# Last feed-forward of a transformer kernel: the turns of the last two z in other PSUM banks, products split in high and low parts, the last tile in halves

## The chip, the core and the metric

The kernel runs on one NeuronCore of a Trainium2 chip. Its time is the device time of one execution in microseconds (us). Five engines work side by side, each on a queue of its own, and meet in semaphores: TensorE (PE in the profile, with PEld for its weight loads), VectorE (DVE), ScalarE (ACT), GpSimd (POOL) and SyncE (SP), which here issues DMAs.

## What is computed

1,024 tokens of width 256 go through two pre-norm transformer layers. The change touches only the end, the second feed-forward, a pair of "bitlinear" layers around a GELU:

```python
def bitlinear(x, w):
    xn = layer_norm(x)
    x_hat = absmax_quant(xn)       # clip(xn * 128 / gamma, -128 + EPS, 128 - EPS) * gamma / 128
    w_hat = ternarize_weights(w)   # -g, 0 or +g
    return einsum('bsd,od->bso', x_hat, w_hat)
y = layernorm(x)
h = gelu(bitlinear(y, w_fc))       # 256 -> 1024
x = x + bitlinear(h, w_proj)       # 1024 -> 256
```

The quantisation does not round, so the operand of the product stays an fp32 number. The kernel splits it into a 16-bit high part and a 16-bit low part and multiplies both with the ternary weights.

## The kernel before, around the change

The tokens are NT = 8 tiles of 128. For each tile t the second feed-forward is this chain, and all of it is written out by hand, as one fixed order for each engine:

- `fc(t)` on PE: eight 128x512 products into banks 0 and 1 (t even) or 2 and 3 (t odd). It waits for the GELU of tile t - 2, which empties these banks.
- `gelu_of(t)` on ACT: GELU out of the two banks, with the row sum kept. It writes `gelu[:, t % 2]` and so waits until `squares(t - 2)` has read it.
- `z_mean(t)` on POOL, then `centre(t)` on ACT: `z[:, t % 2]` = gelu minus its mean. `squares(t)` on ACT: the sum of squares, which `z_factor(t)` on POOL turns into the scale of the result.
- `quantise_z(t)` on DVE: four instructions, absolute maximum, scale, reciprocal, and the product clipped from above, in place in z.
- `z_transposes(t)` on PE, called the turn of z(t) here: eight 128x128 transposes into banks 4 and 5, always these two. So it waits for `zT_lo_done` of tile t - 1, the last reader of the banks.
- `z_high(t)` on ACT copies banks 4 and 5 to `zT_hi[:, t % 2]` as fp16. `z_low(t)` on DVE takes the banks again, clips from below and subtracts the high part: `zT_lo[:, t % 2]`.
- `pj(t)` on PE: sixteen 128x256 products, high and low by turns, into bank 6 or 7 by the list RING. It waits for `zT_lo_done` of tile t before the first of them.
- `result(t)` on DVE: scaled product plus the residual. SP then stores the tile.

The order on PE in the last stage:

```python
z_transposes(0); fc(2); fc(3)
pe.wait_ge(gelu_done, 4)
x_transposes(3, 1, 0)              # tiles 4 to 7 of y, banks 2 and 3
for t in range(1, NT):
    z_transposes(t)
    side(STEPS + 3, f"pj{t - 1}")  # pj(t - 1)
    if t + 3 < NT: fc(t + 3)
side(STEPS + 3, f"pj{NT - 1}")
```

`x_transposes(3, 1, 0)` needs `quantise(1)` on DVE, the quantisation of y  for tiles 4 to 7, part of what the change calls the outer norm. `y_low(1, 2)` is its low part, and `fc(4)` to `fc(7)` need it. On DVE the order is `quantise(1)`, `quantise_z(1)`, `z_low(0)`, `y_low(1, 2)`, and then for t from 2 on `quantise_z(t)`, `z_low(t - 1)`, `result(t - 2)`. ACT runs for t from 3 on `centre(t)`, `gelu_of(t + 1)`, `z_high(t - 1)`, `squares(t)`.

The turns are line L1616 of the profile, all products L1248 (a helper), `x_transposes` L1264, `z_high` L774, `gelu_of` L782, `centre` L790, `squares` L797, `quantise_z` L1203 to L1207, `z_low` L1187, `y_low` L1180, `quantise` L1160 to L1165, `result` L1196, and `z_factor` L545 to L553.

Of the kernel before, what the change touches and what calls it, by code (L numbers as in the profile page):

```python
# [19 lines left out]
ALU = mybir.AluOpType  # L20
# [3 lines left out]
P = 128  # L24
# [3 lines left out]
Q_B = 128.0  # L28
# [3 lines left out]
def transformer_program(nc, x_in, wq_a, wk_a, wv_a, wo_a, w_gate_up, w_down,  # L32
                        wq_b, wk_b, wv_b, wo_b, w_fc, w_proj, cos_in, sin_in, out):
    T, C = x_in.shape[1], x_in.shape[2]
    NT = T // P
    KC = C // P
    F = w_down.shape[1]
    NF = F // P
# [16 lines left out]
    identf = sb("identf", 24, [P], F32)  # L55
# [36 lines left out]
    pjT = sb("pjT", 100.5, [KC, NF, P], F16)  # L92
# [41 lines left out]
    z = sb("z", 146, [2, F], F32)  # L134
    zT_hi = sb("zT_hi", 154, [2, NF, P], F16)
    zT_lo = sb("zT_lo", 158, [2, NF, P], F16)
# [30 lines left out]
    with ExitStack() as ctx:  # L167
        PS = ctx.enter_context(nc.psum_tensor("PS", [P, 8 * BANK], F32))

        def bank(b, n=1):  # L170
            return PS[:, b * BANK:(b + n) * BANK]
# [92 lines left out]
        STEPS = 8 * NG  # L264
# [9 lines left out]
        def blocks(G, part):  # L274
            r = of_step(G)[3]
            return 4 - r if part else 5 + r

        def q_tile(G, part):
            return blocks(G, part) - 1
# [42 lines left out]
        def side_bank(G, name):  # L322
            return 6 + RING.index((G, name)) % 2
# [250 lines left out]
        def _(act):  # L574
            def x_high(st, hf, c, b):

                act.wait_ge(xT_done, 4 * st + 2 * hf + c + 1)
                dst = (yT_hi if st == 3 else xnT_hi)[:, c, hf * BANK:(hf + 1) * BANK]
                nc.scalar.copy(dst, bank(b)).then_inc(xT_hi_done, 1)
# [191 lines left out]

            def z_high(t):
                act.wait_ge(zT_done, t + 1)
                nc.scalar.copy(zT_hi[:, t % 2], bank(4, 2).rearrange("p (i n) -> p i n", i=NF)).then_inc(zT_hi_done, 1)  # L774

            def gelu_of(t):

                act.wait_ge(fc_done, t + 1)
                act.wait_ge(gelu_scale_done, t // 4 + 1)
                if t >= 2:  # L780
                    act.wait_ge(z_squares_done, t - 1)
                nc.scalar.activation(gelu[:, t % 2, :], bank(2 * (t % 2), 2), ACT.Gelu, scale=bit[:, 3, t:t + 1],  # L782
                                     accum_out=bit[:, 8, t:t + 1]).then_inc(gelu_done, 1)
# [8 lines left out]

            def squares(t):

                if t:
                    act.wait_ge(z_squares_done, t)
                nc.scalar.activation(square[:], gelu[:, t % 2, :], ACT.Square, bias=bit[:, 9, t:t + 1],  # L797
                                     accum_out=bit[:, 10, t:t + 1]).then_inc(z_squares_done, 1)
# [15 lines left out]
            squares(2)  # L814
            for c in range(KC):
                x_high(3, 1, c, 2 + c)
            z_high(1)
            for t in range(3, NT):
                centre(t)
                if t + 1 < NT:  # L820
                    gelu_of(t + 1)
                z_high(t - 1)
                squares(t)
            z_high(NT - 1)


        @block.vector
        def _(dve):
# [322 lines left out]
            def y_centre(t):  # L1151
                dve.wait_ge(moments_done, 3 * NT + t + 1)
                nc.vector.tensor_scalar(y[:, t, :], x[:, TAIL_TILES[t], :], mean_of(3, t), None,
                                        ALU.subtract).then_inc(y_centred, 1)
# [29 lines left out]
            def z_low(t):  # L1184

                dve.wait_ge(zT_hi_done, t + 1)
                nc.vector.scalar_tensor_tensor(out=zT_lo[:, t % 2], in0=bank(4, 2).rearrange("p (i n) -> p i n", i=NF),  # L1187
                                               scalar=-Q_B, in1=zT_hi[:, t % 2], op0=ALU.max,
                                               op1=ALU.subtract).then_inc(zT_lo_done, 1)

            def result(t):
# [34 lines left out]
            tail_moments(7)  # L1226
            y_centre(6)
            y_centre(7)
            quantise(1)
            quantise_z(1)  # L1230
            z_low(0)
            y_low(1, 2)
            gelu_scale(1)
            for t in range(2, NT):
                quantise_z(t)
                z_low(t - 1)
                result(t - 2)
            z_low(NT - 1)
            result(NT - 2)
            result(NT - 1)  # L1240

# [2 lines left out]
        def _(pe):  # L1244
# [365 lines left out]

            def z_transposes(t):
                pe.wait_ge(z_done, t + 1)
                if t >= 1:
                    pe.wait_ge(zT_lo_done, t)
                for i in range(NF):
                    last = nc.tensor.transpose(bank(4, 2)[:, i * P:(i + 1) * P], z[:, t % 2, i * P:(i + 1) * P],  # L1616
                                               identf[:])
                last.then_inc(zT_done, 1)

            def pj(t, b):  # L1620
                pe.wait_ge(zT_lo_done, t + 1)
                product(bank(b)[:, 0:C], [(zT[:, t % 2, i, :], pjT[:, :, i, :])
                                          for i in range(NF) for zT in (zT_hi, zT_lo)]).then_inc(pj_done, 1)

            for G in range(STEPS):
                scores(G, 0)
# [17 lines left out]
            z_transposes(0)  # L1644
            fc(2)
            fc(3)
            pe.wait_ge(gelu_done, 4)
            x_transposes(3, 1, 0)
            for t in range(1, NT):
                z_transposes(t)  # L1650
                side(STEPS + 3, f"pj{t - 1}")
                if t + 3 < NT:
                    fc(t + 3)
            side(STEPS + 3, f"pj{NT - 1}")


# [33 lines left out]
```

## Time and profile before

| | us |
|---|---|
| median of 3 runs (616.26 to 617.71) | 616.76 |
| the profiled execution, its own time | 617.08 |
| its span, first to last instruction | 615.3 |
| the stretch of the span from the first turn of z(1) to the end | 579.17 to 615.3 |

The trace is of one execution. All positions are microseconds from the start of its span. In rows of a timeline the first two columns are start and duration, and the bracket is how long the engine was idle before, and what ended this. Durations of successive instructions can overlap a little. A matmul's end is modelled. In rows of the view by stretches, each engine has its busy time and its count of instructions in that stretch, and PEclk is the clock that was granted to TensorE, 1.00 for 2.4 GHz and 0.50 for 1.2 GHz.

### The profile page before, as it was taken

To read this page: it belongs to the slowest core of one execution; us is meant where nothing else is said; L and a number is where in the kernel's file an instruction comes from. 1 tells how busy PE (TensorE), PEld (TensorE's weight loads), DVE (VectorE), ACT (ScalarE), POOL (GpSimd) and SP (SyncE) were. 2 spreads that over 40 slices of the span, in tenths; PEclk is the share of its full clock that TensorE was granted. 3 is DMA by queue.
4 is the path that set the end of the run, shared out by engine and by line. 5 is a ranking of instruction groups with operands and counts; after the bars stand their busy time and mean duration, and the time that the engine had idled before them with its cause. 6 is when DMAs were issued, how large, how long until landed. Compare 5 with 4: busy or idle time off the path is not lost.

```text
span 615.3 us, 16325 instructions
## 1 busy us (share of the span) xinstructions
PE 560.4 (91%) x6880; PEld 484.4 (79%) x6880; DVE 458.6 (75%) x750; ACT 436.2 (71%) x607; POOL 451.6 (73%) x371
## 2 busy tenths in 40 slices
PE   5999999988979999999999999999999987978796
PEld 4878898976758888888878889888888876866474
DVE  4686767767767878777877888788788775765985
ACT  0624302168787889889779898888988888874684
POOL 3034336438997998998999899899999887872332
PEclk9999999998998999999999999999999999997799
DMA  8160004008999999999999999999999999994011
GB/s 286 58 205 0 2 23 89 2 2 145 202 163 187 180 183 207 194 189 179 210 188 191 207 191 203 196 186 211 186 188 182 199 207 189 183 195 88 1 34 36
DMA packets 317193, 91.76 MB, mean 149 GB/s; under 512 B 305984, under 2 KB 316224, under 8 KB 317120
## 3 DMA queue, kind: packets, MB, share of 16 engines
q1 hardware_dynamic: 311680, 86.66, 81.2%
q10 hardware_dynamic: 5440, 4.06, 2.6%
q8 instruction: 54, 0.88, 0.6%
q14 instruction: 19, 0.16, 0.1%
HBM read 13.11 MB, written 1.05 MB: 23 GB/s over the span
## 4 chain that ended last, share of the span: by engine, by line
PE 33%; POOL 24%; DMA 13%; DVE 13%; ACT 7%; SPq 5%; issue 5%; POOLq 0%; ACTq 0%; DVEq 0%
POOL p_lo L497 17%; DMA pT_lo<-p_lo 12%; PE PS L1248 10%; PE PS L1507 4%; DVE small L1078 4%; PE PS L1381 3%; POOL roped L486 3%; SPq L398 3%; PE PS L1527 3%; ACT probs L711 2%; PE PS L1358 2%; PE PS L1363 2%; PE PS L1359 2%; SPq L402 2%; POOL roped L483 2%
## 5 line engine op out<-in xcount | busy, mean ns | idle before, releaser
L497 POOL TENSOR_TENSOR p_lo<-probs,p_hi 128x2048 f16<-128x2048 f32 (+7 forms) x128 | 304.3, 2400 | 34.8 <-DMA pT_lo<-p_lo 20.3
L711 ACT ACTIVATE probs<-PS,small 128x128 f32<-128x128 f32 (+7 forms) x256 | 173.5, 743 | 46.0 <-DVE small L1078 42.7
L1078 DVE TENSOR_REDUCE small<-PS 128x2 f32<-128x2048 f32 (+7 forms) x128 | 172.7, 1350 | 20.9 <-PE PS L1507 20.3
L720 ACT CAST p_hi<-probs 128x2048 f16<-128x2048 f32 (+7 forms) x128 | 145.9, 1161 | 3.8 <-DMA pT_hi<-p_hi 3.8
L1527 PE MATMUL PS<-v_hi,pT_hi 128*128 128x65 f16 x1152 | 78.7, 195 | 2.1 <-DMA pT_hi<-p_hi 2.1
L1531 PE MATMUL PS<-v_lo,pT_hi 128*128 128x64 f16 x1152 | 78.6, 195 | 0.0
L1507 PE MATMUL PS<-k_hi,q_hi 64*128 64x512 f32 (+3 forms) x384 | 74.8, 385 | 2.9 <-ACT probs L711 2.9
L1527 PEld LDWEIGHTS PS<-v_hi,pT_hi 128*128 128x128 f16 x1152 | 73.8, 99 | 3.8 <-issue 2.2
L1531 PEld LDWEIGHTS PS<-v_lo,pT_hi 128*128 128x128 f16 x1152 | 72.4, 98 | 0.6
L1507 PE MATMUL PS<-k_lo,q_hi 64*128 64x512 f32 (+3 forms) x384 | 67.2, 344 | 0.0
L1507 PE MATMUL PS<-k_hi,q_lo 64*128 64x512 f32 (+3 forms) x384 | 66.9, 343 | 0.0
L1248 PE MATMUL PS<-wkq_hi,xnT_hi 128*128 128x320 f32 x128 | 44.1, 344 | 9.2 <-DVE t_sin L1026 3.0
L1527 PE MATMUL PS<-v_hi,pT_lo 128*128 128x65 f16 x1152 | 46.1, 195 | 6.9 <-DMA pT_lo<-p_lo 6.9
L1507 PEld LDWEIGHTS PS<-k_hi,q_hi 64*128 64x128 f32 x384 | 36.6, 186 | 15.2 <-ACT probs L711 4.7
L486 POOL TENSOR_TENSOR roped<-t_cos,t_sin 128x256 f32<-128x256 f32 x64 | 47.9, 748 | 0.0
L459 POOL TENSOR_TENSOR hT_lo<-h,hT_hi 128x512 fp32r<-128x512 f32 x16 | 23.6, 1476 | 32.7 <-DVE hT_hi L938 32.7
L1527 PEld LDWEIGHTS PS<-v_hi,pT_lo 128*128 128x128 f16 x1152 | 39.6, 98 | 8.2 <-DMA pT_lo<-p_lo 8.0
L1493 PE MATMUL PS<-masked,picked 128*128 128x128 bf16 x256 | 36.4, 224 | 5.7 <-ACT probs L711 4.1
L1507 PEld LDWEIGHTS PS<-k_lo,q_hi 64*128 64x128 f32 x384 | 37.0, 188 | 3.5
L1248 PE MATMUL PS<-wkq_hi,xnT_lo 128*128 128x320 f32 x128 | 39.6, 309 | 0.0
L1248 PE MATMUL PS<-wkq_lo,xnT_hi 128*128 128x320 f32 x128 | 39.6, 309 | 0.0
L619 ACT ACTIVATE silu<-PS 128x512 f32<-128x512 f32 x16 | 9.6, 598 | 42.1 <-PE PS L1363 42.1
(204 smaller groups left out, 1337.0 us busy)
## 6 DMA issues: line engine op xcount, KB each, us to landing
wgu_nat<-L_ffn_w_gate_up SPq DMA_DIRECT2D x2, 1024.0 KB, 9.2
wo_nat<-L_attn_wo ACTq DMA_DIRECT2D x7, 256.0 KB, 3.2
wkq_nat<-L_attn_wq ACTq DMA_DIRECT2D x6, 256.0 KB, 4.8
x<-L_attn_x SPq DMA_DIRECT2D x4, 256.0 KB, 3.8
wdn_nat<-L_ffn_w_down SPq DMA_DIRECT2D x1, 1024.0 KB, 10.9
wfc_nat<-L_ffn_w_fc SPq DMA_DIRECT2D x1, 1024.0 KB, 5.3
wpj_nat<-L_ffn_w_proj SPq DMA_DIRECT2D x1, 1024.0 KB, 7.6
pT_hi<-p_hi SPq DMA_TRANSPOSE x64, 5.6
```

Of the source, the lines that this page charges most:

```text
L398: sp.dma_start(pT_hi[G % 3][:], p16_hi[G % 2][:], transpose=True).then_inc(pT_hi_landed[G % 3], 16)
L459: nc.gpsimd.tensor_tensor(hT_lo[:, n, :], h32[:, n % 3, :], hT_hi[:, n, :].bitcast(F32), ALU.subtract).then_inc(h_lo_done, 1)
L486: nc.gpsimd.tensor_tensor(roped[:, t, P:3 * P], t_cos[b][:, 1:5, :].rearrange("p h d -> p (h d)"), t_sin[b][:, 1:5, :].rearrange("p h d -> ...
L497: nc.gpsimd.tensor_tensor(p16_lo[G % 2][:, cols], probs[G % 2][:, cols], p16_hi[G % 2][:, cols], ALU.subtract).then_inc(p_lo_done, 1)
L711: nc.scalar.activation(probs[G % 2][:, start:start + w], PS[:, src:src + w], ACT.Exp, bias=nmax[:, 4 * (G % 2) + u:4 * (G % 2) + u + 1]).t ...
L720: nc.scalar.copy(p16_hi[G % 2][:, cols], probs[G % 2][:, cols]).then_inc(p_hi_done, 1)
L1078: nc.vector.tensor_reduce(nmax[:, first:first + 2], both_heads(G, part), AX.X, ALU.max, negate=True).then_inc(nmax_done, 1)
L1248: last = nc.tensor.matmul(dst, lhsT, rhs, start=n == 0, stop=n == len(pairs) - 1)
L1493: ended = nc.tensor.matmul(b[:, at % BANK:at % BANK + P], picked[:], masked[:], start=start, stop=stop, skip_group_check=True)
L1507: last = nc.tensor.matmul(dst[a], q[rows_of[a], q_cols], k[rows_of[a], cols], start=m == 0 and not (part == 0 and ends), stop=m == 2 and n ...
L1527: last = nc.tensor.matmul(o[:, u:u + HEAD + 1], p_block, v_hi[:, j, g, :], start=first, stop=False, skip_group_check=True)
L1531: nc.tensor.matmul(o[:, u:u + HEAD], p_block, v_lo[:, j, g * HEAD:(g + 1) * HEAD], start=False, stop=False, skip_group_check=True)
```

## The change

1. The turns of z(6) and z(7) go to banks 0, 1 and 2, 3. They no longer wait for the low part of the tile before. Instead each waits for the GELU of its own tile, which empties those banks.
2. The last turn raises its semaphore after four of its eight transposes as well, and its high and low parts are made in halves.
3. The products of z(6) and z(7) are issued as eight high ones and then eight low ones. The high ones need only the high part. The turn of z(7) stands between the high and the low ones of z(6). Each of these products now has a wait in front of it.
4. On DVE, `z_low(0)` moves ahead of `quantise(1)`. On PE, `pj(0)` moves ahead of `x_transposes(3, 1, 0)`, and `fc(4)` follows the turn of z(1) at once.
5. On ACT, `squares(3)` moves ahead of `z_high(1)`. `squares(6)` moves behind `centre(7)` and `z_high(6)`, and `squares(7)` stands ahead of the last high parts. `squares` gets a wait for the mean.

```diff
--- before.py
+++ after.py
@@ -274,6 +274,10 @@
         def blocks(G, part):
             r = of_step(G)[3]
             return 4 - r if part else 5 + r
+
+        def z_bank(t):
+
+            return {NT - 2: 0, NT - 1: 2}.get(t, 4)
 
         def q_tile(G, part):
             return blocks(G, part) - 1
@@ -771,7 +775,15 @@
 
             def z_high(t):
                 act.wait_ge(zT_done, t + 1)
-                nc.scalar.copy(zT_hi[:, t % 2], bank(4, 2).rearrange("p (i n) -> p i n", i=NF)).then_inc(zT_hi_done, 1)
+                nc.scalar.copy(zT_hi[:, t % 2], bank(z_bank(t), 2).rearrange("p (i n) -> p i n", i=NF))\
+                  .then_inc(zT_hi_done, 1)
+
+            def last_z_high(k):
+
+                half = slice(k * NF // 2, (k + 1) * NF // 2)
+                act.wait_ge(zT_done, NT + k)
+                nc.scalar.copy(zT_hi[:, (NT - 1) % 2, half], bank(z_bank(NT - 1) + k).rearrange("p (i n) -> p i n", n=P))\
+                  .then_inc(zT_hi_done, 1)
 
             def gelu_of(t):
 
@@ -792,6 +804,7 @@
 
             def squares(t):
 
+                act.wait_ge(z_mean_done, t + 1)
                 if t:
                     act.wait_ge(z_squares_done, t)
                 nc.scalar.activation(square[:], gelu[:, t % 2, :], ACT.Square, bias=bit[:, 9, t:t + 1],
@@ -814,14 +827,20 @@
             squares(2)
             for c in range(KC):
                 x_high(3, 1, c, 2 + c)
+            squares(3)
             z_high(1)
-            for t in range(3, NT):
+            for t in range(3, NT - 1):
                 centre(t)
-                if t + 1 < NT:
-                    gelu_of(t + 1)
+                gelu_of(t + 1)
                 z_high(t - 1)
-                squares(t)
-            z_high(NT - 1)
+                if 3 < t < NT - 2:
+                    squares(t)
+            centre(NT - 1)
+            z_high(NT - 2)
+            squares(NT - 2)
+            squares(NT - 1)
+            last_z_high(0)
+            last_z_high(1)
 
 
         @block.vector
@@ -1184,8 +1203,18 @@
             def z_low(t):
 
                 dve.wait_ge(zT_hi_done, t + 1)
-                nc.vector.scalar_tensor_tensor(out=zT_lo[:, t % 2], in0=bank(4, 2).rearrange("p (i n) -> p i n", i=NF),
+                nc.vector.scalar_tensor_tensor(out=zT_lo[:, t % 2],
+                                               in0=bank(z_bank(t), 2).rearrange("p (i n) -> p i n", i=NF),
                                                scalar=-Q_B, in1=zT_hi[:, t % 2], op0=ALU.max,
+                                               op1=ALU.subtract).then_inc(zT_lo_done, 1)
+
+            def last_z_low(k):
+
+                half = slice(k * NF // 2, (k + 1) * NF // 2)
+                dve.wait_ge(zT_hi_done, NT + k)
+                nc.vector.scalar_tensor_tensor(out=zT_lo[:, (NT - 1) % 2, half],
+                                               in0=bank(z_bank(NT - 1) + k).rearrange("p (i n) -> p i n", n=P),
+                                               scalar=-Q_B, in1=zT_hi[:, (NT - 1) % 2, half], op0=ALU.max,
                                                op1=ALU.subtract).then_inc(zT_lo_done, 1)
 
             def result(t):
@@ -1226,16 +1255,17 @@
             tail_moments(7)
             y_centre(6)
             y_centre(7)
+            z_low(0)
             quantise(1)
             quantise_z(1)
-            z_low(0)
             y_low(1, 2)
             gelu_scale(1)
             for t in range(2, NT):
                 quantise_z(t)
                 z_low(t - 1)
                 result(t - 2)
-            z_low(NT - 1)
+            last_z_low(0)
+            last_z_low(1)
             result(NT - 2)
             result(NT - 1)
 
@@ -1610,17 +1640,41 @@
 
             def z_transposes(t):
                 pe.wait_ge(z_done, t + 1)
-                if t >= 1:
+                if z_bank(t) != 4:
+                    pe.wait_ge(gelu_done, t + 1)
+                elif t >= 1:
                     pe.wait_ge(zT_lo_done, t)
                 for i in range(NF):
-                    last = nc.tensor.transpose(bank(4, 2)[:, i * P:(i + 1) * P], z[:, t % 2, i * P:(i + 1) * P],
-                                               identf[:])
-                last.then_inc(zT_done, 1)
+                    turned = nc.tensor.transpose(bank(z_bank(t), 2)[:, i * P:(i + 1) * P], z[:, t % 2, i * P:(i + 1) * P],
+                                                 identf[:])
+                    if i == NF - 1 or t == NT - 1 and i == NF // 2 - 1:
+                        turned.then_inc(zT_done, 1)
 
             def pj(t, b):
                 pe.wait_ge(zT_lo_done, t + 1)
                 product(bank(b)[:, 0:C], [(zT[:, t % 2, i, :], pjT[:, :, i, :])
                                           for i in range(NF) for zT in (zT_hi, zT_lo)]).then_inc(pj_done, 1)
+
+            def pj_high(t):
+                b = side_bank(STEPS + 3, f"pj{t}")
+                emptied(STEPS + 3, f"pj{t - 2}")
+                for i in range(NF):
+                    if t < NT - 1:
+                        pe.wait_ge(zT_hi_done, t + 1)
+                    else:
+                        pe.wait_ge(zT_hi_done, NT + 2 * i // NF)
+                    nc.tensor.matmul(bank(b)[:, 0:C], zT_hi[:, t % 2, i, :], pjT[:, :, i, :], start=i == 0, stop=False)
+
+            def pj_low(t):
+                b = side_bank(STEPS + 3, f"pj{t}")
+                for i in range(NF):
+                    if t < NT - 1:
+                        pe.wait_ge(zT_lo_done, t + 1)
+                    else:
+                        pe.wait_ge(zT_lo_done, NT + 2 * i // NF)
+                    last = nc.tensor.matmul(bank(b)[:, 0:C], zT_lo[:, t % 2, i, :], pjT[:, :, i, :], start=False,
+                                            stop=i == NF - 1)
+                last.then_inc(pj_done, 1)
 
             for G in range(STEPS):
                 scores(G, 0)
@@ -1644,14 +1698,21 @@
             z_transposes(0)
             fc(2)
             fc(3)
+            side(STEPS + 3, "pj0")
             pe.wait_ge(gelu_done, 4)
             x_transposes(3, 1, 0)
-            for t in range(1, NT):
+            z_transposes(1)
+            fc(4)
+            for t in range(2, NT - 1):
                 z_transposes(t)
                 side(STEPS + 3, f"pj{t - 1}")
                 if t + 3 < NT:
                     fc(t + 3)
-            side(STEPS + 3, f"pj{NT - 1}")
+            pj_high(NT - 2)
+            z_transposes(NT - 1)
+            pj_low(NT - 2)
+            pj_high(NT - 1)
+            pj_low(NT - 1)
 
 
 # ---- launch: one core; inputs and outputs as the reference has them ----
```

## Rows read from the trace of the kernel before

**Rows 1.** Chain that ended last, in order of time: start, us, what.
```profile
577.89 1.14 DVE zT_lo L1187
...
579.17 1.94 PE PS L1616 x8
581.11 4.93 PE PS L1248 x24
...
591.27 3.47 PE PS L1248 x24
...
605.75 1.23 DVE zT_lo L1187
...
607.12 1.08 PE PS L1616 x8
...
609.26 1.24 DVE zT_lo L1187
...
610.63 1.92 PE PS L1248 x16
...
612.65 0.48 DVE x L1196
```

**Rows 2.** Stretches: busy time (x instructions) of PE, PEld, DVE, ACT, POOL; PEclk; DMA.
```profile
573.70:577.10 3.40, 1.22 (x9) 0.86 (x8) 3.23 (x10) 3.40 (x6) 2.20 (x5) 1.00 0.00 0
...
579.10:584.00 4.90, 4.83 (x23) 3.93 (x24) 4.58 (x8) 2.06 (x2) 0.00 (x0) 0.50 0.01 3
...
601.60:607.10 5.50, 2.92 (x25) 2.40 (x25) 4.97 (x8) 3.96 (x6) 2.54 (x8) 1.00 0.08 26
```

**Rows 3.** Timeline of PE, 573 to 602 us.
```profile
575.99 1.09 PE L1264 MATMUL PS<-identf,y 128*128 128x128 f32 x8 [2.16 <-ACT gelu L782]
...
598.93 1.04 PE L1616 MATMUL PS<-identf,z 128*128 128x128 f32 x8
599.80 0.27 PE L1248 MATMUL PS<-pjT,zT_hi 128*128 128x256 f16 x1
...
601.44 0.27 PE L1248 MATMUL PS<-pjT,zT_lo 128*128 128x256 f16 x1
```

**Rows 4.** Timeline of ACT, 576 to 609 us.
```profile
576.97 1.05 ACT L579 CAST yT_hi<-PS 128x512 f16<-128x512 f32 x2
...
586.09 1.11 ACT L782 ACTIVATE gelu<-PS,bit 128x1024 f32<-128x1024 f32 x1 [2.88 <-PE PS L1248]
...
597.92 1.14 ACT L790 ACTIVATE z<-gelu,bit 128x1024 f32<-128x1024 f32 x1
599.13 1.12 ACT L782 ACTIVATE gelu<-PS,bit 128x1024 f32<-128x1024 f32 x1
...
600.23 1.00 ACT L774 CAST zT_hi<-PS 128x1024 f16<-128x1024 f32 x1
601.12 1.16 ACT L797 ACTIVATE square<-gelu,bit 128x1024 bf16<-128x1024 f32 x1
...
602.27 1.14 ACT L790 ACTIVATE z<-gelu,bit 128x1024 f32<-128x1024 f32 x1
```

**Rows 5.** Timeline of DVE, 572 to 604 us.
```profile
572.78 1.22 DVE L1160 TENSOR_REDUCE bit<-y 128x4 f32<-128x1024 f32 x1
...
578.94 1.28 DVE L1180 SCALAR_TENSOR_TENSOR yT_lo<-PS,yT_hi 128x512 f16<-128x512 f32 x2
...
582.57 1.22 DVE L1187 SCALAR_TENSOR_TENSOR zT_lo<-PS,zT_hi 128x1024 f16<-128x1024 f32 x1
...
599.09 1.22 DVE L1203 TENSOR_REDUCE bit<-z 128x1 f32<-128x1024 f32 x1 [0.43 <-ACT z L790]
...
602.53 0.48 DVE L1196 SCALAR_TENSOR_TENSOR x<-PS,bit,x 128x256 f32<-128x256 f32 x1
```

**Rows 6.** Timeline of POOL: the scale of the last result.
```profile
606.10 0.19 POOL L545 TENSOR_SCALAR bit<-bit 128x1 f32<-128x1 f32 x1 [2.37 <-ACT square L797]
...
607.03 0.34 POOL L553 TENSOR_SCALAR bit<-bit,small 128x1 f32<-128x1 f32 x1
```

**Rows 7.** Groups by line, 579 to 615.3 us: busy us, mean ns | idle before.
```profile
L1248 PEld LDWEIGHTS PS<-pjT,zT_lo 128*128 128x128 f16 x64 | 6.7, 104 | 1.1
```

## Prediction

> **What bounds the kernel now.** I read three things: the chain of waits that ended last, backwards from the end [rows 1]; the busy time and clock by stretches [rows 2]; and the timelines of PE, ACT, DVE and POOL in the last 40 us [rows 3 to 6]. The reader should see three stages.
>
> *Start, up to 586 us.* PE does little from 573.70 to 577.10 (1.22 of 3.40 us busy), and its clock is 1.00 there and 0.50 from 579.10 to 584.00 [rows 2]. The first turn, of z(1), waits for `z_low(0)`, which ends at 579.03 [rows 1]. Then PE runs without a gap, turn, `pj(0)`, `fc(4)`: 1.94 + 4.93 us, to 586.05. ACT idles 2.88 us for `fc(4)` before `gelu_of(4)` [rows 4]. So the start is bound by PE at the low clock, with `pj(0)` in front of `fc(4)`.
>
> *Middle, 586 to 601 us.* One tile costs PE 0.87 for the turn (598.93 to 599.80, rows 3) and 3.47 for the products [rows 1], 4.34 us, without idle time. ACT needs 1.10 for the GELU (start of 599.13 to start of 600.23), 0.89 for the high part, 1.15 for the squares (to 602.27), and 1.05 for the centre (its 1.14 less 0.09, by which successive instructions overlap), about 4.2 [rows 4]. DVE needs 3.44 for `quantise_z` and `z_low` (599.09 to 602.53), of which `z_low` is 1.13 (1.22 less 0.09) and `quantise_z` 2.31, and 0.4 for `result`, about 3.85 [rows 5]. PE sets the pace, ACT is just below it.
>
> *End, from 601.6 us.* No `fc` is left, and what is left runs one after the other: z(7) is centred only after `squares(6)` (602.27), quantised from about 603.4, its turn waits for `z_low(6)` (605.75 + 1.23, turn at 607.12), then the high part, `z_low(7)` at 609.26, sixteen products at 610.63, `result(7)` at 612.65 [rows 1, 4]. From 598.93 (the turn of z(5), rows 3) to `result(7)` it is 13.72 us.
>
> **The change, part by part.** I lay the new order out again with durations from the rows. Start-to-start times at full clock: turn 0.87, eight 128x256 products 0.87 (15 steps from 599.80 to 601.44, so 0.109 each) [rows 3], `fc` 3.47 - 1.74 = 1.73. From a producer's end to a waiting engine's start: 0.14 for DVE to PE (579.03 to 579.17, rows 1).
>
> *Start.* `z_low(0)` ahead of `quantise(1)`: it takes the place at 572.75 and ends at 573.97. `quantise(1)`, which started at 572.78, shifts by 1.13, `quantise_z(1)` too, and `y_low(1, 2)` follows as before at 578.94, since the same instructions stand in front of it [rows 5]. On DVE the move costs nothing. On PE, `pj(0)` starts at 574.1 in what was idle time (2.16 us before 575.99, rows 3), at full clock (1.00, rows 2), and ends by 576.0. `x_transposes` waited for `gelu_of(3)` and for y; the last tile of y now comes at about 576.7, so both copies to yT_hi end about 0.1 later than 578.02 [rows 4], before `y_low` asks for them. The turn of z(1) waited for `z_low(0)` until 579.03; now z(1) itself is done at about that time (577.89 + 1.13), so the turn starts at 579.16: nothing gained. Then `fc(4)` comes at once. With the low clock as before: turn to 580.9, seven of eight products at twice 0.216 us, the last at full rate, end about 584.07. Then the next wait is near: the turn of z(2) needs `z_low(1)`, at 582.57 + 1.22 + 0.14 = 583.93 [rows 5]. So if the clock stays full and `fc(4)` ends at 582.1, the turn of z(2) still starts at 583.9. It starts at 584.07 or 583.93, against 585.88 (586.05 less the overlap of its duration). I take 584.07, gain **1.81**; the other end is 1.95.
>
> `squares(3)` moved in front of `z_high(1)`: 1.15 us in ACT's idle time between 578.1 and the end of the turn at about 581.1 [rows 1, 4]: free; without this cover it would delay `z_high(1)`, and so `z_low(1)`, by up to 1.15. All it gives is that ACT needn't do it after `gelu_of(4)`.
>
> *Middle.* Same work in the same order, PE at 4.35 a tile, three tiles, all shifted by 1.81. PE's nearest waits have slack. `gelu_of(4)` starts at 586.09 - 1.81 = 584.28, `z_high(2)` at 585.38, `z_low(2)` 1.04 later at 586.42 and PE may use it 1.36 later: at 587.8 for a turn at 588.42. In the same way the low part of z(3) is there at 592.1 for 592.77, and that of z(4) at 596.6 for 597.12. Gain 0.
>
> *End.* The turn of z(5) is at 597.12, `gelu_of(7)` at 597.32, `centre(6)` at 596.12 and `quantise_z(6)` at 597.29 (all rows of before less 1.81, rows 3 to 5; `gelu_of(6)` ends 0.09 into the next instruction at 594.1). From there:
> - Turn of z(6): its z is ready for PE at 597.29 + 2.31 + 0.09 + 0.14 = 599.83, PE is free at 599.74. It doesn't wait for `z_low(5)` (599.6 to 600.82, a PE start at 600.96), as it did before. Gained 1.13.
> - `centre(7)` at 599.33, straight after `gelu_of(7)` and `z_high(5)`, ready at 600.50; `squares(6)` no longer stands in between. DVE comes to it only at 601.15 (`quantise_z(6)` to 599.59, `z_low(5)` to 600.72, `result(4)`). So DVE is late next. `quantise_z(7)` 601.15 to 603.45, z(7) written at 603.55.
> - `z_high(6)` at 600.93, `squares(6)`, `squares(7)` to 604.13, both in ACT's wait. `z_low(6)` 603.45 to 604.67, so PE may use it at 604.81.
> - PE: `pj(5)` 600.96 to 602.70, high products of z(6) to 603.57, turn of z(7) 603.69 to 604.56. Before, this turn waited for `z_low(6)`; now it runs during it.
> - First half of the last turn seen by ACT at 604.35; half a high part 0.58 and half a low part 0.69, both by 128x512 rows (1.05 for two, 1.28 for two; rows 4, 5): high halves end at 604.93 and 605.43, low halves (DVE has `result(5)` to 604.98 first) at 605.67 and 606.28, so PE may use the last at 606.42.
> - PE: low products of z(6) from 604.81, high of z(7) from 605.69, low of z(7) from 606.56 (its waits are over at 606.42), so 24 x 0.109 without a gap. `result(7)` starts 2.02 us after the first of the last sixteen (610.63 to 612.65): 605.69 + 2.02 = **607.71**.
> - The scale for `result(7)` now follows `squares(7)`: 604.2 plus the 1.27 us of POOL's three instructions (606.10 to 607.37, rows 6), well before 607.7. The added wait in `squares` is for a mean that is there since 598.9. The wait for the GELU at both moved turns is over at 594.1 and 598.5.
>
> From the turn of z(5) to `result(7)` that is 10.59 against 13.72, gain **3.13**. After `result(7)` nothing changes (612.65 to the end at 615.3).
>
> The waits in front of single products: 24 of them are on the path. The nearest row with waits inside a run of transposes is L1264, four waits more, 1.09 against 1.04 to 1.08 for eight [rows 1, 3]: 0 to 0.013 us each, 0 to 0.3 in all. I take 0.1.
>
> Sum: 1.81 + 3.13 - 0.1 = **4.84 us** against the profiled execution's 617.08 (span 615.3 plus 1.78 outside it), 612.2; against the median, 0.32 lower, **611.9 us**.
>
> **The rivals.**
>
> *A. The clock takes part back.* The low clock followed 1.22 us of work in 3.40 [rows 2] and cost half of the 4.83 busy us run in it. In the new order, if the clock is full at 579.1, PE is done with `fc(4)` by 582.1 and idles until 583.9, after having idled from about 577.4 to 579.16. If the clock falls around 584 instead of 577, then the turn of z(2), `pj(1)` and `fc(5)` run low. These are the pace. For it: idle times of about this size stood before the fall of before [rows 2, 3]. Against it: 2.92 us of work in 5.50 kept 1.00 in the end of before [rows 2]. Price: 4.83 / 2 = 2.4 for a stretch as long as that one, less for a shorter; time up to 614.3. The Trainium skill, in "TensorE: Matmul & The Clock Gate", section "A second HAM failure mode: psum-queue depth-cycling", says that a kernel that cycles through PSUM banks can idle PE for short spells between groups of products and lose time to a clock that swings. By that rule this rival would be the case, and the time near 614; the end of this trace, where PE idled 2.58 of 5.50 us between its turns, shows no fall [rows 2].
>
> *B. The waits break the product stream (slower).* Each of the 32 split products has its own wait. If it kept a weight load from running under the product before, each would cost 0.104 [rows 7] + 0.27 - 0.109 = 0.27 us more: the high products of z(6) would end at 605.7, delay the last turn by 2.0, and 24 x 0.27 = 6.4 come on top, 8.4 in all: 3.5 us slower than before, about 620.3. It decides at about 0.18 us a wait. Against it: 0.013 at most in L1264, whose waits stand in the same place.
>
> *C. The change doesn't do what it says.* Both parts fail: the start is eaten by A twice over, or ACT, only 0.15 a tile below PE, becomes the pace. A loss of 3.6 us or more would be needed: 615.6 to 617.
>
> **How the numbers follow.** Forecast 0.70, A 0.21, B 0.04, C 0.05. The likeliest case's own range is 611.0 to 612.7 (start 0.15 better, waits 0.3, and half a microsecond by which runs of before differ from their median). The range goes up over most of A: 610.9 to 614.0. A difference under 0.2% (1.2 us) can't be told from none here. Faster 0.91, same 0.04, slower 0.05.
>
> **What would show it.** Products of z(0) in PE's timeline at about 574.1; a wait of about 0.1 or less between `fc(4)` and the turn of z(2); the turn of z(2) at about 584.0; turns of z(5), z(6), z(7) at 597.1, 599.8, 603.7; 24 products from 604.8 without a gap; `result(7)` at 607.7. Wrong would be: PEclk of 0.50 after 584 (A), steps over 0.109 between split products (B), or a turn of z(6) that starts with `pj(5)` behind it late because `quantise_z(6)` is late (ACT has become the pace, C).

## The result, and the profile after

The changed kernel takes 610.60 us (median of 6 runs, 607.96 to 612.61) against 616.51 for the kernel before (median of 6, 615.62 to 617.72): a ratio of 0.9911, 95% interval 0.9886 to 0.9935. In a second set of runs it was 611.06 against 615.10, 0.9929 (0.9903 to 0.9955). The forecast was 611.9, between 610.9 and 614.0, worked out from 616.76 for the kernel before. As a time, 610.60 lies 0.3 us under the lower end. As a ratio it lies inside: 0.9911 of 616.76 is 611.3, and the forecast was a ratio of 0.992. Both intervals leave out 1, so the changed kernel is faster, by 0.7 to 0.9%.

The profiled execution took 610.31 us, its span is 608.5. The chain that ended last, in order of time (start, us, what), answers to [rows 1]:

```profile
571.28 1.13 DVE zT_lo L1206
...
582.35 1.07 PE PS L1648 x8
583.42 3.47 PE PS L1278 x24
...
595.58 0.87 PE PS L1648 x8
596.46 1.75 PE PS L1278 x16
598.20 0.93 PE PS L1648 x8
...
599.26 1.91 PE PS L1278 x16
601.17 0.87 PE PS L1666 x8
602.04 0.91 PE PS L1648 x8
...
603.00 1.05 PE PS L1675 x8
604.04 0.87 PE PS L1666 x8
604.92 0.89 PE PS L1675 x8
...
605.91 0.48 DVE x L1225
```

In [rows 1] the end went back and forth between DVE, PE and ACT. Here it is PE's own line of work from 582.35 to the last result: the turns are L1648, the high products L1666, the low ones L1675, the other products L1278. Of DVE and ACT nothing stands in the chain behind the turn of z(2) but the last result. From the turn of z(5) to the last result PE is busy for 10.22 of 10.50 us:

```profile
595.40:605.90 10.50, 10.22 (x89) 8.58 (x87) 9.12 (x15) 7.67 (x12) 4.11 (x10) 1.00 0.12 42
```

The stretches of time that answer to [rows 2] (columns as there):

```profile
573.70:577.10 3.40, 2.22 (x16) 1.38 (x13) 3.23 (x10) 3.40 (x7) 1.14 (x3) 1.00 0.02 5
577.10:579.10 2.00, 1.61 (x9) 1.32 (x10) 2.00 (x5) 0.72 (x3) 0.33 (x1) 0.73 0.00 0
579.10:584.00 4.90, 4.54 (x23) 2.50 (x22) 4.73 (x9) 3.75 (x5) 0.52 (x3) 0.76 0.08 27
```

TensorE's clock still falls, but later, and less work runs under it. Its timeline there:

```profile
577.49 1.52 PE L1648 MATMUL PS<-identf,z 128*128 128x128 f32 x8 [1.54 <-DVE z L1236]
578.80 0.63 PE L1278 MATMUL PS<-fcT,yT_hi 128*128 128x512 f16 x1
...
581.61 0.38 PE L1278 MATMUL PS<-fcT,yT_lo 128*128 128x512 f16 x1
582.35 1.07 PE L1648 MATMUL PS<-identf,z 128*128 128x128 f32 x8 [0.36 <-DVE zT_lo L1206]
```

The first turn waits for z(1) itself, no longer for the low part of z(0). `fc(4)` follows it, six of its eight products at the low clock (0.63 us each, against 0.38 for the last). Then the turn of z(2) waits 0.36 us for the low part of z(1). DVE's timeline shows why: it works on without an idle time that the profile marks, from the first row here to the last.

```profile
570.69 0.58 DVE L1172 TENSOR_SCALAR y<-x,moments 128x256 f32<-128x256 f32 x2
571.19 1.22 DVE L1206 SCALAR_TENSOR_TENSOR zT_lo<-PS,zT_hi 128x1024 f16<-128x1024 f32 x1
572.33 1.21 DVE L1179 TENSOR_REDUCE bit<-y 128x4 f32<-128x1024 f32 x1
...
576.68 0.75 DVE L1236 TENSOR_SCALAR z<-z,bit 128x1024 f32<-128x1024 f32 x1
577.35 1.28 DVE L1199 SCALAR_TENSOR_TENSOR yT_lo<-PS,yT_hi 128x512 f16<-128x512 f32 x2
...
580.98 1.22 DVE L1206 SCALAR_TENSOR_TENSOR zT_lo<-PS,zT_hi 128x1024 f16<-128x1024 f32 x1
```

The first of these rows is used as the mark from here on. It is the centring of y, the last step ahead of everything that the change moves. In the kernel before it stands here:

```profile
572.17 0.58 DVE L1153 TENSOR_SCALAR y<-x,moments 128x256 f32<-128x256 f32 x2
```

From it to the start of the last result ("the stretch" from here on) it is 612.65 - 572.17 = 40.48 us before and 605.91 - 570.69 = 35.22 after: 5.26 less. The rest of the 6.8 us by which the spans differ (1.48 us ahead of the mark, 0.06 behind) lies almost all in the first part, where the two kernels do the same work in the same order. In the 14 traces of this case, of both kernels and of all experiments, the mark stands anywhere from 569.55 to 573.40, whichever kernel it is. This spread of 3.85 us is of the size by which executions of one kernel differ (2 to 6 us from fastest to slowest within a set of six or more). Only profiled executions have a mark, so it isn't shown that the two are the same thing. Two traces of the changed kernel (below) differ by 1.21 us in time and by 1.16 in the mark. So the experiments are read by the stretch, which repeats to 0.01 us in the changed kernel, and by the median only where it can tell. Each stretch is that of one trace.

### The profile page after: what moved, and what is told of

The parts are those of the page before. It is cut to its first block, busy times and chain, and to the rows that moved or that the text cites. A ratio compares the mean times of both kernels' runs of the same rounds, so it can differ in the third digit from the quotient of the medians.

```text
span 608.5 us, 16334 instructions
## 1 busy us (share of the span) xinstructions
PE 557.9 (92%) x6880; PEld 481.3 (79%) x6880; DVE 458.2 (75%) x751; ACT 436.8 (72%) x608; POOL 452.5 (74%) x371
## 4 chain that ended last, share of the span: by engine, by line
PE 41%; POOL 18%; DVE 16%; DMA 11%; ACT 6%; SPq 4%; issue 4%; POOLq 0%; ACTq 0%; DVEq 0%
POOL p_lo L501 13%; PE PS L1278 12%; DMA pT_lo<-p_lo 10%; PE PS L1537 7%; DVE small L1097 6%; PE PS L1557 4%; PE PS L1411 3%; SPq L402 3%; ACT probs L715 2%; POOL roped L490 2%; PE PS L1388 2%; PE PS L1393 2%; PE PS L1389 2%; PE PS L1301 2%; PE PS L1561 2%
## 5 line engine op out<-in xcount | busy, mean ns | idle before, releaser
L1278 PE MATMUL PS<-wkq_hi,xnT_hi 128*128 128x320 f32 x128 | 43.8, 342 | 8.7 <-DVE oT_lo L1112 2.8
L1278 PE MATMUL PS<-wkq_lo,xnT_hi 128*128 128x320 f32 x128 | 39.6, 309 | 0.0
L1278 PE MATMUL PS<-wkq_hi,xnT_lo 128*128 128x320 f32 x128 | 39.5, 308 | 0.0
L1523 PEld LDWEIGHTS PS<-masked,picked 128*128 128x128 bf16 x256 | 16.6, 97 | 28.7 <-issue 14.5
```

The source lines that it names most:

```text
L1278: last = nc.tensor.matmul(dst, lhsT, rhs, start=n == 0, stop=n == len(pairs) - 1)
L1523: ended = nc.tensor.matmul(b[:, at % BANK:at % BANK + P], picked[:], masked[:], start=start, stop=stop, skip_group_check=True)
```

## Experiments

**Either half alone.** `start_only` is the kernel before with the edits of the start (and the wait for the mean in `squares`):

```diff
+            side(STEPS + 3, "pj0")
             pe.wait_ge(gelu_done, 4)
             x_transposes(3, 1, 0)
-            for t in range(1, NT):
+            z_transposes(1)
+            fc(4)
+            for t in range(2, NT):
...
+            z_low(0)
             quantise(1)
             quantise_z(1)
-            z_low(0)
...
+            squares(3)
             z_high(1)
...
-                squares(t)
+                if t > 3:
+                    squares(t)
```

> The kernel before with the edits of the start alone (low part of z(0) and its products moved ahead, fc(4) straight after the turn of z(1), squares(3) moved). Measured by the stretch from the two centrings of y on DVE to the start of the last result, 40.48 us in the kernel before and 35.22 in the changed one. Theory (start and end add up, each is what the sum said): about 2.0 us off this stretch, so 38.5, and a ratio of about 0.997. Rival (the gain of the start only moves the wait to ACT's order or the banks further down, and is worth nothing without the end): about 40.2.

Measured: stretch 38.46, and 614.54 us in the median of 12 runs against 615.10, ratio 0.9987 (0.9969 to 1.0005). This interval holds 1, so the medians don't show the 2.02 us that the stretch shows. Its first turn and that of z(2) stand where they do in the changed kernel (6.80 and 11.65 us behind the mark). Its end is that of before, with the same two waits for a low part, and a third before the last products:

```profile
595.32 1.04 PE L1619 MATMUL PS<-identf,z 128*128 128x128 f32 x8
599.16 1.06 PE L1619 MATMUL PS<-identf,z 128*128 128x128 f32 x8 [1.06 <-DVE zT_lo L1190]
603.51 1.06 PE L1619 MATMUL PS<-identf,z 128*128 128x128 f32 x8 [1.54 <-DVE zT_lo L1190]
607.03 0.27 PE L1251 MATMUL PS<-pjT,zT_hi 128*128 128x256 f16 x1 [0.71 <-DVE zT_lo L1190]
```

`end_only` is the changed kernel with these edits undone:

```diff
-            side(STEPS + 3, "pj0")
             pe.wait_ge(gelu_done, 4)
             x_transposes(3, 1, 0)
-            z_transposes(1)
-            fc(4)
-            for t in range(2, NT - 1):
+            for t in range(1, NT - 1):
...
-            z_low(0)
             quantise(1)
             quantise_z(1)
+            z_low(0)
...
-            squares(3)
             z_high(1)
...
-                if 3 < t < NT - 2:
+                if t < NT - 2:
                     squares(t)
```

> The changed kernel with the edits of the start undone. Theory: the stretch is 3.1 to 3.2 us shorter than before, so 37.3, ratio about 0.995. Rival (the two parts need each other, the end's gain comes only if ACT is ahead): under 2 us, so over 38.5.

Measured: stretch 36.58, 613.46 us in the median of 12 runs against 615.10, ratio 0.9961 (0.9940 to 0.9982). The stretch is 0.7 shorter than expected, and not because of the end:

```profile
599.30 1.04 PE L1647 MATMUL PS<-identf,z 128*128 128x128 f32 x8
601.92 1.09 PE L1647 MATMUL PS<-identf,z 128*128 128x128 f32 x8
```

From the turn of z(5) at 599.30 to the last result at 609.79 it takes 10.49 us. In the changed kernel it is 605.91 - 595.42 = 10.49 too, and it was 13.72 before. The 0.7 lie in the start: the turn of z(2) came at 13.05 behind the mark and not at 13.71. So the two halves add up (2.02 from `start_only`, 3.24 from the end here, 5.26 together), and the start of before isn't the same in each run.

**Both kernels a second time.** No edit.

> The changed kernel unaltered, for a second trace. Theory: the stretch from the centrings of y to the last result is 35.2 again within 0.2, and what the whole time differs by from run to run lies ahead of this stretch. Rival: the spread of the changed kernel (608.0 to 612.6) is in this stretch, from TensorE's clock falling at other places.

> The kernel before unaltered, for a second trace. Theory: in its start TensorE sets the pace at the low clock, so its stretch from the centrings of y to the last result varies with where the clock rises, from 39.5 to 41; from the turn of z(5) to the last result it is 13.7 again. Rival: 40.5 again within 0.1, as the changed kernel's 35.2 is.

Measured: the changed kernel's stretch is 35.22 again, with the mark at 571.85 instead of 570.69. That of before is 40.06 (from 570.18 to 610.24); turn of z(5) to last result 13.73. Here are stretches of time and TensorE's timeline of the changed kernel, second trace (its mark is 1.16 us later than in the first, so the same positions lie 1.16 us earlier in the work):

```profile
577.10:579.10 2.00, 0.46 (x5) 0.46 (x5) 1.90 (x5) 1.83 (x4) 0.47 (x2) 1.00 0.00 0
579.10:584.00 4.90, 3.02 (x19) 1.64 (x18) 4.80 (x10) 3.27 (x4) 0.71 (x4) 1.00 0.00 0
```

```profile
578.65 1.09 PE L1648 MATMUL PS<-identf,z 128*128 128x128 f32 x8 [1.54 <-DVE z L1236]
579.94 0.38 PE L1278 MATMUL PS<-fcT,yT_hi 128*128 128x512 f16 x1 [0.20 <-DVE yT_lo L1199]
...
583.50 1.06 PE L1648 MATMUL PS<-identf,z 128*128 128x128 f32 x8 [1.68 <-DVE zT_lo L1206]
```

And the second trace of before:

```profile
577.10:579.10 2.00, 1.90 (x9) 1.85 (x10) 2.00 (x4) 0.00 (x0) 0.00 (x0) 0.50 0.00 0
579.10:584.00 4.90, 4.90 (x30) 3.32 (x28) 4.52 (x9) 2.39 (x3) 0.00 (x0) 0.80 0.08 27
```

```profile
583.47 1.04 PE L1616 MATMUL PS<-identf,z 128*128 128x128 f32 x8
```

This time the changed kernel kept the full clock, `fc(4)` was through 1.3 us earlier (`gelu_of(4)` at 10.01 behind the mark, not 11.34), and the turn of z(2) stood where it stood before, at 11.65: it only waited 1.68 us instead of 0.36. In the kernel before the clock was low in both traces, but rose earlier against the work in the second, and all of that showed: turn of z(2) at 13.29 instead of 13.71, stretch 0.42 shorter. This answers both expectations: the stretch of the changed kernel stays, that of the kernel before moves with the clock.

**Rival A, the clock.** `filled_idle` puts work that nobody needs into TensorE's idle time:

```diff
             x_transposes(3, 1, 0)
+            pe.wait_ge(x_added, 8 + wo_count(NG - 1, 3))
+            for i in range(14):
+                nc.tensor.transpose(bank(side_bank(STEPS + 3, "pj1"))[:, 0:P], identf[:], identf[:])
             z_transposes(1)
```

> The changed kernel with fourteen 128x128 transposes of the identity, needed by nothing, in TensorE's idle time ahead of the turn of z(1), about 1.5 us. Theory: the clock stays at 1.00 there, fc(4) ends up to 1.7 us earlier, and still the turn of z(2) comes at 11.65 us after the centrings of y, since it waits for the low part of z(1); the stretch stays at 35.2. Rival A of the prediction (the clock decides): the stretch is 0.5 us or more shorter.

Measured: stretch 35.21, clock 1.00 from 576 to 586.

```profile
576.33 1.69 PE L1706 MATMUL PS<-identf 128*128 128x128 f32 x14
578.03 1.09 PE L1648 MATMUL PS<-identf,z 128*128 128x128 f32 x8
579.32 0.38 PE L1278 MATMUL PS<-fcT,yT_hi 128*128 128x512 f16 x1 [0.20 <-DVE yT_lo L1199]
...
582.88 1.06 PE L1648 MATMUL PS<-identf,z 128*128 128x128 f32 x8 [1.68 <-DVE zT_lo L1206]
```

The turn of z(2) waits the same 1.68 us for DVE as in the second trace above. That the added work held the clock up isn't shown, since that trace kept 1.00 without it. Nine traces have the new start up to the turn of z(2), and in all nine this turn stands 11.64 to 11.66 behind the mark, five times with a low clock ahead of it and four times (this one among them) without. What the clock still costs comes behind that turn, and only where it stays low so long: in `last_tile_whole` below it was low from 581.9 to about 585.4, and the turn of z(3) came 0.13 us later than at full clock (16.16 behind the mark against 16.03); in `one_pair_of_banks` it was 0.06.

**Rival B, the waits.** `waits_everywhere` puts a wait that is already satisfied ahead of each product of z(0) to z(5) too:

```diff
-                product(bank(b)[:, 0:C], [(zT[:, t % 2, i, :], pjT[:, :, i, :])
-                                          for i in range(NF) for zT in (zT_hi, zT_lo)]).then_inc(pj_done, 1)
+                for n, (zT, i) in enumerate([(zT, i) for i in range(NF) for zT in (zT_hi, zT_lo)]):
+                    pe.wait_ge(zT_lo_done, t + 1)
+                    last = nc.tensor.matmul(bank(b)[:, 0:C], zT[:, t % 2, i, :], pjT[:, :, i, :], start=n == 0,
+                                            stop=n == 2 * NF - 1)
+                last.then_inc(pj_done, 1)
```

> The changed kernel with a wait, already satisfied, in front of each of the sixteen products of z(0) to z(5) as well, 90 more than now. The products of z(1) to z(4) stand in a stretch in which TensorE sets the pace. Theory (a satisfied wait costs 0 to 0.013 us): a tile of that stretch stays at 4.35 us, at most 4.55, and the stretch from the centrings of y to the last result stays under 36.1. Rival B of the prediction (0.27 us a wait): 4.3 us more a tile, the stretch over 50.

Measured: stretch 35.21. The products of z(2):

```profile
587.39 0.27 PE L1657 MATMUL PS<-pjT,zT_hi 128*128 128x256 f16 x1
587.50 0.27 PE L1657 MATMUL PS<-pjT,zT_lo 128*128 128x256 f16 x1
...
589.02 0.27 PE L1657 MATMUL PS<-pjT,zT_lo 128*128 128x256 f16 x1
```

Fifteen steps in 1.63 us, 0.109 each, as in [rows 3]. A satisfied wait costs nothing that shows. The waits did reach the chip: in this trace the weight loads of all 128 products of z carry a semaphore wait, in the changed kernel those of 38. The 90 between them are the 90 of the expectation.

**The end, one edit undone at a time.** `one_pair_of_banks`, `products_interleaved`, `last_tile_whole` and `squares6_in_front`:

```diff
-            return {NT - 2: 0, NT - 1: 2}.get(t, 4)
+            return 4
```

```diff
-            pj_high(NT - 2)
             z_transposes(NT - 1)
-            pj_low(NT - 2)
-            pj_high(NT - 1)
-            pj_low(NT - 1)
+            side(STEPS + 3, f"pj{NT - 2}")
+            last_pj()                      # sixteen by turns, waits for the low part half by half
```

```diff
-            last_z_high(0)
-            last_z_high(1)
+            z_high(NT - 1)
...
-            last_z_low(0)
-            last_z_low(1)
+            z_low(NT - 1)
...                                    # on PE, one semaphore for the whole turn, and the products wait for all of it
```

```diff
-            centre(NT - 1)
-            z_high(NT - 2)
             squares(NT - 2)
+            centre(NT - 1)
+            z_high(NT - 2)
             squares(NT - 1)
```

> The changed kernel with all eight turns in banks 4 and 5, so that the last two wait for the low part of the tile before again. Measured by the stretch from the centrings of y to the last result, 35.22 us in the changed kernel. Theory: the turn of z(6) comes 1.2 us later and that of z(7) too, the high products of z(7) after that, so the last result is 0.95 us later, 36.2. Rival (the split products alone cover the wait): 35.4 or less.

> The changed kernel with the products of z(6) and z(7) high and low by turns again, so that those of z(6) all wait for its low part and come after the turn of z(7). Theory: eight products (0.87 us) fall out of TensorE's idle time, the last result is 0.9 us later, 36.15. Rival (the end is bound by the chain of DVE and ACT and not by TensorE): under 0.2, so 35.4.

> The changed kernel with the last tile's turn, high part and low part whole. Theory: the high part at 31.19 + 1.11, the low part 1.04 later, TensorE has it 1.36 after that, at 34.7 instead of its 34.06, so the last result is 0.65 us later, 35.85. Rival (TensorE is busy with other products until then): 35.25.

> The changed kernel with squares(6) back in front of centre(7) on ACT. Theory: z(7) is ready 1.15 us later, 0.5 to 0.65 us of this show at its quantisation on DVE and at the last result: 35.75 to 35.9. Rival (DVE is late anyway by all of it): 35.25.

Measured (the third column leaves out what the start differs by):

| | stretch | turn of z(5) to last result | more than 10.49 | expected more |
|---|---|---|---|---|
| one pair of banks | 36.26 | 11.48 | 0.99 | 0.95 |
| products by turns | 36.16 | 11.44 | 0.95 | 0.9 |
| last tile whole | 35.92 | 11.06 | 0.57 | 0.65 |
| squares(6) in front | 35.73 | 11.02 | 0.53 | 0.5 to 0.65 |

The four add up to 3.04, against 3.23 us for the whole end. Each was undone with the others in place, so they needn't add up to it exactly, and the 0.19 stay open. The traces show where each loss lies. With one pair of banks, the turn of z(6):

```profile
599.10 1.06 PE L1648 MATMUL PS<-identf,z 128*128 128x128 f32 x8 [1.06 <-DVE zT_lo L1206]
```

With the products by turns, the turn of z(7) comes no later than in the changed kernel (31.17 behind the mark), and TensorE idles 0.69 us until then, in which the high products of z(6) could run:

```profile
603.37 1.09 PE L1648 MATMUL PS<-identf,z 128*128 128x128 f32 x8 [0.69 <-DVE z L1236]
```

With `squares(6)` in front, the same turn comes 31.68 behind the mark, 0.49 later than in the changed kernel, because z(7) does:

```profile
603.85 1.10 PE L1648 MATMUL PS<-identf,z 128*128 128x128 f32 x8 [0.34 <-DVE z L1236]
```

With the last tile whole, DVE waits for all of the high part:

```profile
606.88 1.22 DVE L1205 SCALAR_TENSOR_TENSOR zT_lo<-PS,zT_hi 128x1024 f16<-128x1024 f32 x1 [0.70 <-ACT zT_hi L778]
```

**Is there more at the start?** TensorE had still idled 1.54 us ahead of the first turn. `reorder_start` fills that with work that is needed:

```diff
             side(STEPS + 3, "pj0")
+            z_transposes(1)
             pe.wait_ge(gelu_done, 4)
             x_transposes(3, 1, 0)
-            z_transposes(1)
+            side(STEPS + 3, "pj1")
             fc(4)
-            for t in range(2, NT - 1):
+            z_transposes(2)
+            fc(5)
+            for t in range(3, NT - 1):
...
             z_low(0)
+            quantise_z(1)
             quantise(1)
-            quantise_z(1)
+            z_low(1)
...
+            z_high(1)
+            centre(3)
             for c in range(KC):
                 x_high(3, 1, c, 2 + c)
             squares(3)
-            z_high(1)
...                                    # z_low(1) and centre(3) fall out of the loops
```

> The changed kernel with one more reordering of the start: quantisation of z(1) ahead of that of y for tiles 4 to 7, turn of z(1) ahead of the transposes of y, low part of z(1) and pj(1) ahead of fc(4), so that TensorE's idle time before the turn of z(1) holds work. Theory (TensorE's work sets the pace up to the end, and idle time filled at the start comes back at the end): 0.7 to 1.0 us off the stretch, so 34.3. Rival (ACT, at 4.2 us a tile against 4.35, takes over at once, and y comes 1.2 us later): 0 to 0.3, so 35 or more.

`reorder_more` goes on from there:

```diff
             fc(5)
+            fc(6)
             for t in range(3, NT - 1):
                 z_transposes(t)
                 side(STEPS + 3, f"pj{t - 1}")
-                if t + 3 < NT:
-                    fc(t + 3)
+                if t == 3:
+                    fc(7)
...
                 gelu_of(t + 1)
-                z_high(t - 1)
                 if 3 < t < NT - 2:
                     squares(t)
+                z_high(t - 1)
```

> The kernel of the reordered start with fc(6) ahead of the turn of z(3), where TensorE idled 1.10 us, and squares(4) and squares(5) ahead of the high part on ACT. Theory: gelu_of(6) and gelu_of(7) come 1 us earlier, of which 0.45 us reach the end, because the turn of z(5) then waits for the low part of z(4): stretch 34.2. Rival (ACT's 4.2 us a tile is the pace now and nothing is left): 34.7.

Measured: stretches 34.68 and 34.24, so 0.54 and 0.98 less than the changed kernel. The first fell between the two expectations: the turn of z(3) waited 1.10 us for the low part of z(2), so of the time filled only a part came back. The second came out as expected, with the turn of z(5) waiting in its place:

```profile
593.32 1.06 PE L1652 MATMUL PS<-identf,z 128*128 128x128 f32 x8 [0.71 <-DVE zT_lo L1208]
```

Their medians are 610.00 us (9 runs, against 615.10; 0.9920, 0.9896 to 0.9945) and 611.19 (7 runs, against 616.91; 0.9912, 0.9879 to 0.9946). Both beat the kernel before. That they beat the changed one is shown by one trace each of the stretch, and not by the medians: 1 us is less than runs differ by.

## Why the prediction was right

*Start, forecast 1.81, with 1.95 as the other end; measured 13.71 - 11.66 = 2.05 between the two first traces, and 13.29 - 11.65 = 1.64 between the second ones.* The step that was wrong is which of two near ends was taken. The prediction let `fc(4)` at the low clock decide (584.07 in its positions; its own terms, 580.9 + 7 x 0.432 + 0.216, give 584.14). It was the low part of z(1) in both traces of the changed kernel. Even with the low clock TensorE had been idle since 11.30 behind the mark, where the prediction has it busy to 11.90, for three reasons: its turn of z(1) started 0.19 earlier against the mark, the clock fell only within this turn (1.31 us to the next start, not 1.74), and six products of `fc(4)` were low, not seven. So the wait was 0.36 and 1.68 us, where the prediction named a wait of 0.1 or less as its sign. DVE was 0.1 us faster than the sum said (10.29 from the mark to the low part of z(1), against 582.57 - 572.17 = 10.40). The reduction of y started 0.61 behind the centring of y, which writes what it reads. `z_low(0)`, which reads nothing of it, starts 0.50 behind it.

The other thing that the prediction hadn't worked out is that the start of before moves with the clock. The turn of z(2) stood at 13.71, 13.29 and, in `end_only`, 13.05. The gain is the difference to a number that varies, while the new start was the same to 0.02 us in nine traces. With the third of these starts it would have been 1.4, so that 1.81 came so near is in part luck. What was said to be free was free in the trace: `z_low(0)`, `pj(0)` (at 572.56, 1.87 behind the mark, forecast 1.9) and `squares(3)`, behind which ACT still idled 1.28 us. These moves were not undone one by one, so what each is worth isn't shown.

*Middle, forecast 0.* From the turn of z(2) to that of z(5) it is 595.42 - 582.35 = 13.07 against 598.93 - 585.88 = 13.05 before.

*End, forecast 3.13 less 0.1 for the waits; measured 3.23.* Steps from the turn of z(5), forecast and measured: turn of z(6) 2.71 and 2.62, turn of z(7) 6.57 and 6.46, low products of z(6) 7.69 and 7.58, last result 10.59 and 10.49. The tenth comes in at the first: z(6) was ready when TensorE got there. The term that was too long is the 0.14 us from DVE to a turn. That is what `z_low` took (579.03 to 579.17). From the last step of `quantise_z` to the turn that waited for it, it was 0.06: 576.68 + 0.75 = 577.43 to 577.49 here, and the same for the turn of z(7) in `products_interleaved` and in `squares6_in_front`. After that each step took what its row said to 0.02 us, and the term for the waits (0.1) was zero. The four experiments give each edit about the price that the order of work gives it, 0.53 to 0.99 us. So the rival that the end is a chain of DVE and ACT, which TensorE's order can't help, falls. DVE and ACT count there too, as `squares(6)` shows with its 0.53.

*Whole.* 4.84 us were forecast. The stretch gave 5.26 and 4.85 in two pairs of traces, and the medians 5.9 and 4.0 in two sets of runs. Where those two differ isn't shown, since medians have no trace. Two things that vary by enough are known: the mark (3.85 us over all traces) and the start of before (0.66).

*Rival A* was right that the clock can fall and wrong in the place and in the price. It supposed a fall around 584, in the idle time behind `fc(4)`, under the turn of z(2), `pj(1)` and `fc(5)`. In no trace of the changed kernel did the clock fall there, though TensorE idled 1.68 us in the second one. Where it fell, it fell between 0.04 us ahead of the turn of z(1) and the middle of `fc(4)`, and the work under it up to the turn of z(2) stood in front of a wait for DVE. In two of the experiments it stayed low past that turn, and cost 0.13 and 0.06 us. A trace of the changed kernel with the fall and one without show the same stretch, 35.22. The Trainium skill, in "TensorE: Matmul & The Clock Gate", section "A second HAM failure mode: psum-queue depth-cycling", tells of a kernel that cycles through PSUM banks and idles TensorE briefly between groups of products, so that the clock swings. These traces don't decide on it. In the end, where three pairs of banks are used, the clock is 1.00, but TensorE is busy for 10.22 of 10.50 us and so hardly has such idle spells. In the start, where the clock falls in some traces, it does fall behind short idle spells, in the banks of before.

*Rival B* is refuted by 90 waits that cost 0.00. The wait at which it would have decided was put too high: 4.84 us over 32 waits is about 0.15, not 0.18. *Rival C*, ACT as the new pace, isn't seen in the changed kernel: its period is 4.35 us, TensorE's.

What stays open: why the part ahead of the mark differs by up to 3.85 us between executions. Between the two traces of the changed kernel it isn't one step. The same instruction of DVE comes 1.03 us earlier in the second trace at 16.09, 1.46 later at 278.23 and 1.16 later at the mark.

## What to carry to other kernels

When an engine's order is written out by hand and its pace is set by TensorE, look at the two ends, where TensorE idles: work that is moved into such a gap can come back at the other end, up to where the next wait ends. `pj(0)` and what went with it brought 1.64 to 2.05 us, and a further reordering into a gap of 1.54 us brought only 0.54, because a turn then waited for DVE. Splitting a sum of products by which operand is ready first, and turning into banks that are free anyway, were worth about 1 us each, as much as their place in the order said. Before an engine's slow clock is blamed or cured, see what waits behind the slow work: here 1.3 us of faster work changed nothing. And measuring from a mark behind the noisy part made differences of a tenth of a microsecond readable in executions that differ by several.

## What the runs showed that was not expected

- The clock of TensorE fell in the start in some executions and not in others of one and the same kernel (1.00 from the mark on in one trace of the changed kernel, 0.50 from about 578 to 581.5 in the other), with the same order of work and, to 0.02 us, the same busy time in each microsecond from 3 behind the mark up to the fall. Five of the nine traces with the new start show a fall, 6.8 to 8.5 us behind the mark, four none.
- A wait on a satisfied semaphore in front of each of sixteen products in a row left their step at 0.109 us. That a product with its own wait streams as well as one without was expected to within 0.013 us, and it is closer than that.
